# A graph network kernel: GpSimd waits twice inside each chunk's gathers until those issued have landed

## What is computed

```python
# layer 1: five GAT passes (four with W_std, the last on [in_x, x] with W_skip)
h = x @ W; al = h @ a_src; ar = h @ a_dst
logit = leaky_relu(al[src] + ar[dst], 0.2)
out = segment_sum(segment_softmax(logit, dst)[:, None] * h[src], dst) + b
# layer 2: one dot pass
e = leaky_relu(sum(k[src] * q[dst], -1), 0.2)
out = segment_sum(f[src] * segment_softmax(e, dst)[:, None], dst)
# layer 3: three passes with four heads ("multi"), which also update the edge features
```

## Time and profile before

| | us |
|---|---|
| median of 3 runs without profile | 10527.93 (10525.65 to 10530.43) |
| span of the profiled execution | 14084.2 |
| GpSimd (POOL) busy in it | 7724.8 (55%) |
| TensorE (PE) busy | 6814.7 (48%) |
| VectorE (DVE) busy | 7042.7 (50%) |
| ScalarE (ACT) busy | 5152.3 (37%) |

### The profile page before, as it was taken

The page is one execution under the profiler, slowest core; times in us unless marked ns, Lnnn a source line. Parts: engine busy times, 40 slices in busy tenths (PEclk is TensorE's granted clock), DMA queues, the critical chain, the costliest instruction groups (busy, mean ns, idle before and its releaser), DMA issues. The chain is left out here.

```text
span 14084.2 us, 100376 instructions
## 1 busy us (share of the span) xinstructions
PE 6814.7 (48%) x27637; PEld 5669.8 (40%) x27637; DVE 7042.7 (50%) x12322; ACT 5152.3 (37%) x5609; POOL 7724.8 (55%) x7576
## 2 busy tenths in 40 slices
PE   5443366657756774777577646661111322232222
PEld 5433355545545553655455535551111211121111
DVE  5333345434444443444444546663444466646666
ACT  0011144444434443444344424442222243423432
POOL 7888755544444445344444455546665555545553
PEclk7555577768777776887677767775555565556555
DMA  5333322212211221122133323333332344434442
GB/s 154 36 36 33 58 51 58 56 39 55 54 49 42 56 55 42 48 55 55 40 90 91 86 72 97 97 89 89 115 109 96 116 143 136 140 94 141 138 140 81
DMA packets 782270, 1137.56 MB, mean 81 GB/s; under 512 B 500471, under 2 KB 559955, under 8 KB 774499
## 3 DMA queue, kind: packets, MB, share of 16 engines
q0 software_dynamic: 355008, 370.44, 14.1%
q1 hardware_dynamic: 363245, 417.03, 9.6%
q10 hardware_dynamic: 63926, 349.09, 6.2%
HBM read 680.14 MB, written 468.70 MB: 82 GB/s over the span
## 5 line engine op out<-in xcount | busy, mean ns | idle before, releaser
L970 POOL DMA_INDIRECT turned<-d_t,idx x5788 | 5465.9, 944 | 5006.3 <-DVE wide L1426 3228.1
L1115 PE MATMUL banks<-pair,hot 128*128 128x462 f32 x16184 | 3981.1, 402 | 1677.0 <-issue 1661.2
L1115 PEld LDWEIGHTS banks<-pair,hot 128*128 128x128 f32 x16184 | 3357.4, 208 | 2299.7 <-issue 1921.1
L1236 DVE TENSOR_TENSOR wide<-banks,member 128x462 f32<-128x462 f32 x1156 | 689.9, 634 | 2788.3 <-remote 2123.6
L1084 ACT COPY wide<-wide 128x952 f32<-128x952 f32 (+2 forms) x252 | 503.4, 1997 | 2831.5 <-DVE wide L1446 2800.7
L650 POOL DMA_INDIRECT d_acc<-work,idx x784 | 1237.7, 1579 | 263.9 <-issue 234.4
L733 ACT ACTIVATE hot<-keys,row 128x1024 fp32r<-128x1024 f32 (+1 forms) x1036 | 1073.1, 1117 | 277.9 <-PE banks L1115 204.9
L1171 PE MATMUL banks<-ident,wide 128*128 128x128 f32 x588 | 163.1, 423 | 1814.2 <-issue 945.2
L1446 DVE TENSOR_TENSOR_SCAN wide<-banks,wide 128x224 f32<-128x224 f32 (+4 forms) x1288 | 1036.9, 871 | 5.8
L1128 PE MATMUL banks<-pair,hot 128*128 128x448 f32 x3136 | 804.7, 417 | 452.1 <-issue 393.8
L1128 PEld LDWEIGHTS banks<-pair,hot 128*128 128x128 f32 x3136 | 688.1, 221 | 568.7 <-issue 492.5
(11 more groups left out here) (311 smaller groups left out, 9556.1 us busy)
## 6 DMA issues: line engine op xcount, KB each, us to landing
d_e<-wide ACTq DMA_DIRECT2D x168, 924.0 KB
turned<-d_t,idx POOLq DMA_INDIRECT x5788
d_e<-wide ACTq DMA_DIRECT2D x84, 1008.0 KB
wide<-d_b SPq DMA_DIRECT2D x60, 1344.0 KB
keys<-d_key SPq DMA_DIRECT2D x124, 512.0 KB
d_b<-wide SPq DMA_DIRECT2D x28, 1344.0 KB
wide<-d_edge SPq DMA_DIRECT2D x84, 448.0 KB
d_em<-wide ACTq DMA_DIRECT2D x84, 448.0 KB
```

The source lines that it names most:

```text
L970: gp.indirect_dma_start(rows[:, b, k, :], None, table[:, :], offset(idx[:, b, k:k + 1])).then_inc(s["gathered"][b], 16)
L1115: mm = nc.tensor.matmul(ps_cols[i], hot[:, place, i, j, :], flat(g.pair[:, part, j]), start=(j, part) == (0, 0), stop=(j, part) == (SETS - ...
L1236: nc.vector.tensor_tensor(found[:, i - i0], ps_cols[i].rearrange("p (w c) -> p w c", c=SET), mid(member[:, i], TW), ALU.mult).then_inc(pic ...
```

## The change

Inside `gather`, in passes that have X > 0 (the five GAT passes and the dot pass), GpSimd waits before gather number KG // 3 and before number 2 * KG // 3 until all gathers that it has issued for this chunk are in SBUF. The short first chunk of GAT passes 2 to 5 is left alone. The multi passes are unchanged.

```diff
-        def gather(t, b, columns):
+        def gather(t, b, columns, later=True):
 
             gp.wait_ge(s["rows_used"][b], t + 1)
             gp.wait_ge(s["idx_ready"][b], t + 1)
 
             gp.sem_inc(s["pool_steps"], 1)
             for k in range(columns):
+                if X and k in (KG // 3, 2 * KG // 3) and columns == KG:
+                    gp.wait_ge(s["gathered"][b], 16 * (KG * t + k) - (16 * X * AH if b == 0 else 0) if later else 16 * k)
+                    gp.sem_inc(s["pool_steps"], 1)
                 gp.indirect_dma_start(rows[:, b, k, :], None, table[:, :],
                                       offset(idx[:, b, k:k + 1])).then_inc(s["gathered"][b], 16)
 
         if X:
-            gather(0, 0, KG - X * AH)
-            gather(0, 1, KG)
+            gather(0, 0, KG - X * AH, False)
+            gather(0, 1, KG, False)
```

## The result

| | kernel before | changed kernel |
|---|---|---|
| median of 4 runs each, us | 10528.74 (10525.65 to 10530.43) | 11313.27 (11307.95 to 11319.86) |
| ratio | | 1.0744, 95% interval 1.0729 to 1.0759 |

The change costs 785 us. The forecast was 11057, with a range up to 11300: the direction held, the size of the wait did not.

A forecast was written before the change was run, and what follows sets the result against it. The prediction took GpSimd's gathers to bound GAT and dot chunks. 208 waits at 1.44 us (300) and 104 at 2.2 (229) gave 529 us on 10528, so 11057; the forecast's own range was 10850 to 11250, the whole range 10560 to 11300.

The forecast's parts named there:

- I take GpSimd as the bound of GAT and dot chunks: GAT and dot chunks, unprofiled: GpSimd sets the pace, 24.96 us against TensorE's 24.1, and 29.95 against VectorE's 29.3.
- So the wait adds 1.44: Each GpSimd wait: 1.74 us from a multi-pass gather's issue to VectorE's start, less the 0.30 gap, adds 1.44 us.
- GAT passes 1 to 4 have a DMA share of 0.20 to 0.22, and there I take 1.44: First four GAT passes: 208 waits at 1.44 us each, 300 us, chosen for their low DMA share.
- there I take the middle of 1.44 and 2.96, 2.2: Last GAT pass and dot pass, DMA share 0.35 and 0.37: 104 waits at 2.2 us each, 229 us.
- The Trainium skill's 2.0 us: Other count for every wait: a fixed 2.0 us per DMA, so 312 waits at 1.70 us cost 530 us.
- Is this stall there without the profile? The time says hardly: TensorE's stall in profiled chunks: hardly present in unprofiled runs, which take 10528 us, 3556 less than the profiled span.
- The second rival: Faster: TensorE's stall exists in small in every run and the waits cut it, at most 249 us, to 10279; chance 0.10.
- the span should not grow by 529; it may even shrink: Profiled span of 14084 us: chunks there are bound by the stalled TensorE, so the waits add about 0.
- Part of the cost hidden: GAT and dot chunks: with a gather pace between 1.06 and 1.248 us, 10550 to 10850 us; chance 0.14.
- all hidden: GAT and dot chunks: GpSimd has room at a pace below 1.06 us a gather, so time stays 10528 us; chance 0.09.
- Each wait costs the upper bound: Third rival: waits land beside stores and key loads, 312 at 2.96 us, 924 us, giving 11452; above 11250 had chance 0.07.
- the signs named: Profile: 328 GpSimd idle stretches before L973 near 1.7 us, longer in last GAT and dot pass; pace 1.248 us; multi unchanged.

## Why the prediction was wrong, by its steps

- **"I take GpSimd as the bound of GAT and dot chunks"**: right on the chip of the comparison for the GAT passes, while in the dot pass VectorE was just ahead (30.5 us, forecast 29.3 of its own work). Waits that don't pause cost 0, fewer gathers save 286 us, and the pauses show in full but for half a microsecond in a dot chunk. TensorE "close behind" in the GAT pass was right as well: 23.5 us without six of the gathers, forecast 24.1.
- **"So the wait adds 1.44"**: this is the step that failed. The 1.74 us were read from a gather's issue to VectorE's start, and GpSimd's own restart was taken to be as prompt, with the gap of 0.30 subtracted. In the trace of the changed kernel VectorE still starts 1.63 us after the issue, but GpSimd 2.27, since it takes 0.78 us from the landing to its next gather. The wait adds 1.97, and the few waits that meet other traffic bring the mean of GAT passes 2 to 4 to 2.1. Over 208 waits of the first four passes 0.53 each is 110 us. By the table, the forecast is short by 73 us in the first pass, 36 in each of the next three, 26 in the fifth and 45 in the dot pass, 252 in all.
- **"GAT passes 1 to 4 have a DMA share of 0.20 to 0.22, and there I take 1.44"**: the mean share was the wrong thing to look at. In the first pass the second wait stands right behind the store and idles GpSimd 3.69 us. That pass gave 148 us for the 75 of the forecast. The earlier trace rows had shown the store's 2.5 us at a share of 0.88; what was missing was to lay it on the gathers' timeline.
- **"there I take the middle of 1.44 and 2.96, 2.2"**: 2.7 and 3.1 a wait were measured in the last GAT pass and the dot pass. The upper bound of 2.96 came from a single gather at the start of a node stage, read again at VectorE's start; single waits idle GpSimd for up to 6.2 us. So the range ended too low.
- **The Trainium skill's 2.0 us** (DMA: Bandwidth & Descriptors, Anatomy of one DMA) would have priced a wait at 1.70 added. Measured were 1.97 in a quiet place and up to 5.9 behind other transfers; it is nearer than the 1.44, and short too.
- **"Is this stall there without the profile? The time says hardly"**: right for this comparison, and wrong in its reason. Recording does not stretch the kernel: three plain chips have spans within 0.1% of the times. The stall goes with the chip (or with its set of runs), and two of five have it in every run.
- **The second rival, "the change cuts it"**: it was given a tenth, and put at 249 us at most. On the plain chips it does not happen. On a stalling chip it is the result, and 1187 us in size. The forecast "the span should not grow by 529; it may even shrink" held for the stalling chips, and the profile after was taken on a plain one, where it grew by 784 us, as the runs did.
- **Part of the cost hidden (0.14), all hidden (0.09)**: neither; GAT intervals grew by what the two pauses add, and the dot pass's by 5.9 of 6.4 us. **"Each wait costs the upper bound"**, 11452: not reached in the mean, but nearer than the forecast (785 us for 312 waits is 2.5 each, between 1.44 and 2.96).
- Of the signs named: all 328 stretches stand in the trace (314 of them under the gathers' DMA, the rest put elsewhere), 2.3 us long in quiet places and not 1.7; pace within a third 1.248 us; multi passes unchanged. All but the length held.

## What to carry to other kernels

A landing wait on the engine that sets the pace costs its whole pause, and the pause is to be read at the restart of the engine that waits, not at another engine's. Lay each wait on the timeline of stores and loads: a wait right behind one costs 1.5 to 3.5 us more than one a few gathers away, and moving a wait can hit another transfer (5.36 us in the mean for 3.27, in the last GAT pass). When a profile's span and the runs' times are a third apart, take neither stall nor cure from the profile until the same kernel has been profiled again where its time is known. A pacing wait that is a loss on one chip can be a gain on the next, so both have to be measured before it is kept or dropped.

## What the runs showed of the hardware

- Chips differ: the same kernel takes 10528 to 10533 us on three and 14060 and 14109 us on two, each steady within 0.3%. Profiled runs take as long as the others of their set.
- On the latter, in GAT passes, after some 13 to 15 us of back-to-back gathers TensorE stands idle 1.5 to 2.5 us before single matmuls, at a clock that had been granted in full. In the two chunks read it recovered 2.1 and 3.7 us after the last of them was issued. Series of 6 and 7 gathers did not bring it on.
- In the second GAT pass's median GpSimd issues its next gather 0.78 us after the landing that it waits for, and VectorE starts 0.13 us after one (in the chunk shown 2.27 and 1.63 us after the issue); a wait that is already met costs nothing (10533, 10527 and 10529 us against 10533, 10528 and 10528).
- A gather issued 0.35 us behind ScalarE's store landed 1.5 us late; one issued while SyncE issued a load for 4.89 us, behind a store, landed 3.5 us late.
